# Turning layer 1's attention probabilities with a DMA transpose, under newly ordered plans

## What is computed

```python
x = x + attn(_ln(x) * (scale1 + 1.0) + shift1) * gamma1
h = _gelu_tanh((_ln(x) * (scale2 + 1.0) + shift2) @ Wfc1.T + bfc1)
x = x + (h @ Wfc2.T + bfc2) * gamma2
# attn: 16 heads of 32 features
qn = q / norm(q) * sm; kn = k / norm(k)
p = softmax(einsum('bhqd,bhkd->bhqk', qn, kn) + attn_bias)
o = einsum('bhqk,bhkd->bhqd', p, v) @ Wproj.T + bproj
```

## Time and profile before

| | us |
|---|---|
| median of 3 runs | 2487.38 (2487.06 to 2489.5) |
| the profiled execution | 2486.12 |
| its span, first to last instruction | 2484.3 |
| mean granted TensorE clock | 0.992 of full speed |

### The profile page before, as it was taken

One profiled execution on the slowest core, in us unless ns is written; L12 is line 12 of the kernel. 1 busy time (PEld: TensorE's weight loads), 2 busy tenths in 40 slices (PEclk: granted clock), 3 DMA queues, 4 the chain that ended last, 5 costly groups with the idle time before them and its releaser, 6 DMA issues.

```text
span 2484.3 us, 46028 instructions
## 1 busy us (share of the span) xinstructions
PE 2427.0 (98%) x17878; PEld 1163.2 (47%) x17878; DVE 1345.1 (54%) x2062; ACT 912.9 (37%) x1496; POOL 999.6 (40%) x943
## 2 busy tenths in 40 slices
PE   7699999999999999999999999999999999999999
PEld 4244444444444444444444444454545444454544
DVE  7474251533415234152575585867757586766752
ACT  3343231322313223132343462625445262644542
POOL 2242231332323223132344354645546464555632
PEclk8899999999999999999999999999999999999999
DMA  8762423314132131333443635334252524425230
GB/s 217 208 146 62 97 48 81 67 39 102 41 89 58 42 99 41 90 65 92 133 103 111 151 84 140 70 101 96 72 140 48 156 54 111 102 73 127 60 83 30
DMA packets 311485, 231.50 MB, mean 93 GB/s; under 512 B 227718, under 2 KB 238342, under 8 KB 311308
## 3 DMA queue, kind: packets, MB, share of 16 engines
q1 hardware_dynamic: 311308, 228.89, 37.1%
HBM read 124.08 MB, written 18.75 MB: 57 GB/s over the span
## 4 chain that ended last, share of the span: by engine, by line
PE 81%; DVE 6%; issue 4%; DMA 3%; POOL 3%; ACT 2%; SPq 1%; POOLq 0%; DVEq 0%; ACTq 0%
PE ps_m L1882 46%; PE ps_abef L1882 17%; PE ps_c L1882 5%; PE ps_d L1882 3%; PE ps_abef L2075 2%; PE ps_abef L2071 2%; PE ps_abef L2069 2%; POOL scratch L1278 1%; PE ps_abef L2105 1%; POOL scratch L1274 1%; PE ps_abef L2113 1%; DVE weights L1571 1%; DMA scratch<-mod 1%; PE ps_abef L2094 1%; PE ps_d L1965 1%
## 5 line engine op out<-in xcount | busy, mean ns | idle before, releaser
L1882 PE MATMUL ps_m<-h_mlp,weights 128*128 128x512 f16 x3168 | 723.1, 380 | 8.0 <-DVE scratch L1709 3.6
L1882 PE MATMUL ps_m<-weights,inner 128*128 128x512 f16 x3072 | 681.4, 379 | 0.3 <-POOL inner L1248 0.3
L1248 POOL TENSOR_TENSOR inner<-scratch,inner 128x512 f16<-128x512 f32 x256 | 303.5, 1191 | 466.7 <-ACT inner L1421 466.2
L1882 PEld LDWEIGHTS ps_m<-h_mlp,weights 128*128 128x128 f16 x3168 | 304.1, 98 | 367.5 <-issue 9.2
L1882 PEld LDWEIGHTS ps_m<-weights,inner 128*128 128x128 f16 x3072 | 297.7, 98 | 352.2 <-POOL inner L1248 0.6
L1882 PE MATMUL ps_abef<-h_mlp,weights 128*128 128x512 f16 x1440 | 330.1, 379 | 0.0
L1222 POOL TENSOR_TENSOR scratch<-scratch 128x512 f16<-128x512 f32 x120 | 141.6, 1180 | 410.9 <-ACT scratch L1374 410.1
L1882 PEld LDWEIGHTS ps_abef<-h_mlp,weights 128*128 128x128 f16 x1440 | 137.4, 98 | 164.8 <-issue 4.2
L1421 ACT CAST inner<-scratch 128x512 f16<-128x512 f32 x256 | 156.8, 613 | 106.9 <-DVE scratch L1716 69.0
L1374 ACT CAST scratch<-scratch 128x512 f16<-128x512 f32 x120 | 74.0, 616 | 313.7 <-DMA h_mlp<-scratch 157.7
L1845 DVE SCALAR_TENSOR_TENSOR scratch<-scratch 128x512 f32<-128x512 f32 x128 | 102.1, 799 | 57.0 <-ACT scratch L1510 56.9
(11 more groups left out here) (172 smaller groups left out, 3041.2 us busy)
## 6 DMA issues: line engine op xcount, KB each, us to landing
scratch<-mod SPq DMA_DIRECT2D x128, 256.0 KB, 4.0
x_mlp<-x_attn SPq DMA_DIRECT2D x64, 256.0 KB, 2.4
weights<-gamma SPq DMA_DIRECT2D x128, 128.0 KB, 3.0
scratch<-scratch SPq DMA_DIRECT2D x128, 128.0 KB, 2.7
scratch<-gain SPq DMA_DIRECT2D x112, 128.0 KB, 2.9
x_attn<-x SPq DMA_DIRECT2D x32, 256.0 KB, 2.9
x_mid<-x_mlp SPq DMA_DIRECT2D x32, 256.0 KB, 2.1
x_attn<-x_mid SPq DMA_DIRECT2D x32, 256.0 KB, 3.1
```

The lines of the kernel that those rows point to most:

```text
L1248: nc.gpsimd.tensor_tensor(inner[:, 1, j, :], src, inner[:, 0, j, :], ALU.subtract).then_inc(L.m_lo, 1)
L1882: ins = nc.tensor.matmul(o, left(a, k), right(b, k), start=(first and n == 0), stop=(last and n == len(order) - 1), skip_group_check=True)
```

## The change

Layer 1's turn_p becomes one DMA transpose on SP, as in layer 0, of 16 blocks of 128x128 from `p1` to `pt1`. The PE transposes and the key_major copies are removed; mix, p_hi, turn and the later `up` steps wait for the DMA's semaphore, or no longer for the copies. All eight order tables, and the lists that place set-up steps, have new numbers.

```diff
+                if stage == "turn_p":
+
+                    cut_done, mixed = counts(tile(it, t) + 1, tile(it, t))
+                    sp.wait_ge(s_cond, 1)
+                    sp.wait_ge(L1.p_lo, cut_done)
+                    sp.wait_ge(L1.mixed, mixed)
+                    sp.dma_start(pt1, p1.rearrange("p g h t -> p (g h t)"), transpose=True).then_inc(L1.pt, 16)
...
-                    act.wait_ge(L1.p_turned, n)
+                    act.wait_ge(L1.pt, 16 * n)
                     nc.scalar.copy(p1[:, :, 0, :], e1).then_inc(L1.p_hi, 1)
-                if stage == "key_major":
-                    act.wait_ge(L1.p_turned, n + 1)
-                    act.wait_ge(L1.mixed, n)
-                    nc.scalar.copy(pt1[:, 0:HALF, :], as16(ps_m[2], HALF)).then_inc(L1.pt, 1)
...
-                if stage == "key_major":
-                    dve.wait_ge(L1.p_turned, n + 1)
-                    dve.wait_ge(L1.mixed, n)
-                    nc.vector.tensor_copy(pt1[:, HALF:, :], as16(ps_m[3], HALF)).then_inc(L1.pt2, 1)
...
                     pe.wait_ge(L1.normed, 2 * n + 2)
-                    pe.wait_ge(L1.pt, n)
-                    pe.wait_ge(L1.pt2, n)
+                    pe.wait_ge(L1.masked, n)
...
-                if stage == "turn_p":
-
-                    pe.wait_ge(L1.p_lo, n + 1)
-                    for g in range(HEADS1):
-                        ins = nc.tensor.transpose(as16(ps_m[2 + g // HALF], HALF)[:, g % HALF, :],
-                                                  p1[:, g].rearrange("p h t -> p (h t)"), ident16[:])
-                    ins.then_inc(L1.p_turned, 1)
                 if stage == "mix":
-                    pe.wait_ge(L1.pt, n + 1)
-                    pe.wait_ge(L1.pt2, n + 1)
+                    pe.wait_ge(L1.pt, 16 * (n + 1))
```

A line of a table, before and after, here the place of `mix` in layer 1's steady plan (one number per tile):

```diff
-    "mix": tiles([46.07, 77.91, 116.14, 175.46]),
+    "mix": tiles([52.35, 94.62, 156.69, 264.35]),
```

More of the change, by code:

```diff
@@ new lines @@
+    "p_lo": tiles([50.24, 98.95, 151.71, 237.61]),
+    "scores": tiles([55.71, 92.42, 146.92, 165.18]),
+    "exp": tiles([65.39, 122.48, 149.43, 177.74]),
+    "shift": tiles([69.22, 96.01, 144.90, 168.13]),
+    "turn_p": tiles([70.02, 102.84, 147.08, 168.14]),
+    "p_hi": tiles([72.34, 131.61, 152.35, 188.90]),
+    "mix": tiles([74.10, 116.87, 164.84, 241.80]),
+    "soft": tiles([74.15, 104.92, 145.84, 177.79]),
+    "out": tiles([83.94, 135.98, 201.19, 297.09]),
+    "c_lo": tiles([84.28, 134.13, 164.78, 257.06]),
@@ new lines @@
+    "flip1": tiles([4.21, 40.42, 47.55, 287.22], 1),
+    "shift": tiles([5.20, 56.42, 89.05, 129.62]),
+    "hi1": tiles([8.06, 40.85, 52.36, 409.32], 1),
+    "p_lo": tiles([17.34, 54.45, 90.81, 147.66]),
+    "soft": tiles([21.77, 57.08, 89.25, 142.84]),
+    "exp": tiles([29.70, 54.78, 89.13, 136.52]),
+    "p_hi": tiles([30.83, 60.21, 94.14, 165.41]),
+    "turn_p": tiles([33.00, 69.24, 132.29, 139.25]),
+    "scores": tiles([34.99, 62.77, 88.92, 139.02]),
+    "c_lo": tiles([43.60, 71.20, 101.37, 170.16]),
@@ L213 @@
[L213 to L216 removed]
+    (-296.14, "ang", 0), (-233.76, "ang", 1), (-187.93, "load", "ada4"), (-167.46, "load", "up0"),
@@ new lines @@
+    "proj": tiles([26.36, 56.64, 81.92, 129.62]),
+    "t_hi": tiles([27.78, 60.41, 92.66, 135.24]),
+    "projv": tiles([37.51, 52.82, 83.88, 134.46]),
+    "spread": tiles([43.53, 81.67, 120.41, 188.18]),
+    "t_lo": tiles([44.63, 61.39, 90.17, 135.33]),
+    "mask": tiles([45.55, 69.84, 101.00, 147.82]),
+    "soft": tiles([47.33, 72.92, 104.82, 180.32]),
+    "turn": tiles([48.11, 76.09, 97.29, 138.86]),
+    "exp": tiles([50.29, 75.28, 104.97, 177.01]),
+    "p_hi": tiles([50.36, 82.02, 122.31, 192.56]),
@@ new lines @@
+    "scores": tiles([52.67, 78.28, 114.41, 143.87]),
+    "p_lo": tiles([53.30, 78.53, 106.98, 173.16]),
+    "c_hi": tiles([57.19, 92.99, 178.86, 300.61]),
+    "c_lo": tiles([58.07, 90.92, 187.27, 238.86]),
+    "add": tiles([69.76, 109.55, 183.78, 303.92]),
+    "weigh": tiles([69.80, 112.27, 206.44, 249.60]),
+    "mix": tiles([71.78, 107.22, 163.81, 313.88]),
+    "turn_p": tiles([71.89, 96.15, 129.02, 182.77]),
+    "stat2": tiles([73.34, 132.88, 215.48, 293.15]),
+    "fetch2": tiles([73.74, 161.82, 196.79, 294.84]),
@@ new lines @@
+    "v_lo": tiles([20.26, 41.40, 72.69, 147.51]),
+    "t_lo": tiles([20.77, 57.07, 108.38, 162.69]),
+    "exp": tiles([22.46, 63.26, 135.82, 188.49]),
+    "mask": tiles([26.05, 62.12, 111.25, 164.71]),
+    "turn": tiles([26.20, 57.63, 105.33, 161.50]),
+    "scores": tiles([29.63, 58.06, 119.66, 183.38]),
+    "soft": tiles([31.41, 65.51, 113.90, 187.10]),
+    "spread": tiles([31.42, 69.24, 137.59, 169.31]),
+    "p_hi": tiles([32.35, 67.29, 153.20, 210.50]),
+    "add": tiles([42.31, 93.88, 162.20, 233.90]),
@@ L463 @@
         "bank d": [("out", "weigh")],
-        "banks e and f": [("turn", "t_lo"), ("scores", "mask"), ("turn_p", "key_major")],
+        "banks e and f": [("turn", "t_lo"), ("scores", "mask")],
         "moments": [("stat1", "scale1"), ("stat2", "scale2")],
```

441 lines of the change are left out of this document (193 added, 248 removed), and 118 rows, old and new, of tables (LAST1_AT, SETUP_START0, SETUP_START1, SETUP_TRANS).

## The result

| | before | after |
|---|---|---|
| median, us | 2487.22 (4 runs, 2486.72 to 2489.50) | 2474.48 (4 runs, 2470.26 to 2479.45) |
| span of the profiled execution | 2484.3 | 2477.7 |
| its granted clock | 0.992 | 0.988 |

The ratio is 0.9948, with a 95% interval of 0.9933 to 0.9963: 12.7 us faster. The forecast was 30.8 us faster, so the sign was right, the size less than half, and the time just inside the upper end of the range (2443 to 2476).

The account below looks back on a forecast made before the run. TensorE was taken to bound the loops: 28.8 us won by the removal, 1 at the start, 2 at the seam, less 1 for late landings, made 2487.4 - 30.8 = 2456.6 us; range 2443 to 2476.

Parts of the forecast that it names:

- What bounds the kernel: In the loops TensorE is the bound, 81% of the chain; work taken off it there is won in full.
- The sum: Removal, start, seam and single late landings: 2486.1 - 28.8 - 1 - 2 + 1 = 2455.3; against the median, 2456.6 us.
- The removal: Layer 1's transposes on TensorE cost 0.90 us a tile; over 32 tiles 28.8 us is won.
- The steady blocks: Layer 1's steady blocks become shorter by 3.6 us each, from 142.9 to 139.3 us.
- The DMA: Layer 1, scores to mix: the 16-block transpose lands in about 4.9 us (4.3 to 6.2); no tile waits.
- (a): Layer 1's transpose lands late, near 6.2 us; waits of 1.5 us a block, 10.5 us: 2467 us; chance 0.17.
- rival (b): Layer 1's transpose lands at 7.8 us; waits eat the gain: 2506 us; chance 0.06, shared with anything else above 2492.
- SyncE's queue: In the steady block, fetch2 3 goes out some 7 us after p_lo, hidden by about 3 us.
- the second of the signs: Sign of being wrong, in SyncE's queue: SP holds a fetch back until scale2 waits for it.
- The block's end: Last out to next block's first up: slack 0.3 us, counted at nothing, at worst 1 us in each of 7 blocks.
- Start and seam: New plans: start -1 us (bounds -6 and +8), 1400 to 1600 us -2 (bounds -6 and +6).
- rival (c): The new start and seam lose their +8 and +6 us instead of winning 3: 2474 us; chance 0.08.

Follow-up runs that it names:

- experiment 6: Also spelled old_no_transpose: order tables of before, layer 1's transposition left out altogether, mix reading untransposed probabilities; 2471.3 us against 2488.9 for the kernel before, 0.9928.
- experiment 8: The changed kernel with 16 idle TensorE transposes per layer 1 tile put back (28.8 us in all): 2495.8 us against 2476.0 for the changed kernel.
- experiment 7: The changed kernel with its DMA transpose left out, mix reading untransposed probabilities: 2474.1 us, the change itself having 2474.5 and 2476.0.
- experiment 4: The changed kernel with mix of tiles 2 and 3 one down step earlier in layer 1's steady plan: 2474.3 us.
- experiment 1: The changed code under the order tables of the kernel before, with only SyncE's order adapted: 2515.3 us, 1.0099 of before.

## Why the prediction was wrong, step by step

**What bounds the kernel.** "So the loops are bound by TensorE: work taken off it there is won in full" was the step that failed, and with it the term of 28.8 us. It was read from idle time: under 1 us in 200. That tells that TensorE is the one that is late now, not how close behind it the next chain is. Under the old tables 2.8 of a steady block's 3.6 us could be taken before VectorE was late, and at the seam nothing. Experiments 6 and 8 price the 28.8 us at 17.6 and 19.8. No rival in the prediction had this.

**The sum.** The forecast had -28.8 for the removal, -3 for start and seam, nothing for the DMA, +1 for single late landings: -30.8. The runs have -17.6 for the removal alone (experiment 6), +2.8 for the new plans (experiment 7 against 6) and +0.4 to +1.9 for the DMA (the change against experiment 7), which is no more than the scatter: -14.4 to -12.9, beside -12.7 measured.

**The removal.** The work was 0.90 us a tile, as read: the distance between block starts, less what the waits add to the usual distance of two matmuls, fell from 142.0 us before to 138.4 in the change and 138.4 in old_no_transpose, 3.6 us for four tiles. But I summed it over all 32 tiles, though 8 of them lie in the seam and the first MLP. The kernel before waits 16.4 us there in all (1195 to 1538 us), and the earlier trace rows had shown 7.8 us of idle time for a part of it. By my own reading ("it stands still mainly at the start and at the seam of the layers") those 7.2 us should not have been counted in full. They gave 1.1 in experiment 6 and 3.4 in the change.

**The steady blocks.** 139.3 us forecast, 140.7 measured. From 142.8 less 3.6 us the missing 1.5 us are, start to start on PE in the change's six blocks: 1.1 for the two outs right behind their mix (seen in the order printed before the prediction, and not priced, though c_hi's copy had to fit between), 0.54 for scores of tiles 1 and 3 (0.32 and 0.22), 0.25 on average at the block's end, less 0.4 by which the waits for tile 0's and tile 1's q and k became smaller. Experiment 4 shows that these are not independent: when the 1.1 went, waits at the block's end, slower matmuls behind them and a new wait of turn took as much on average.

**The DMA.** Landing 4.9 taken, 4.3 measured, at the lower end of 4.3 to 6.2. The rooms were right within 0.5 us. The rivals (a) and (b), late landings, did not occur in the steady blocks, and the one landing of 6.3 us at the seam had twice that room. The Trainium skill (VectorE: DVE Perf Modes, "The three transpose paths") gives 1309 ns for one 128x128 transpose by DMA. As a price for each block of a batch the measurement decides against it: 16 blocks in one DMA landed in 4.3 us, 0.27 a block. Waits for the transpose that eat the gain, which is how rival (b) costs time, came in experiment 1, in the steady blocks for want of room and not by late landings.

**SyncE's queue.** I summed issue times and let the fetch go out 7 us after p_lo, hidden by 3. It went out 8.9 us after, since the store and the hand-over ahead of it wait for others, and the scale stands at the edge: it waits up to 1.3 us in the change and 2.73 in experiment 4. This is the second of the signs that the prediction named for being wrong. **The block's end** was counted at 0 with slack 0.3 and up to 1 us at worst. In the change it cost 0.6 and 0.9 us in two of six blocks, up to 2.4 in experiment 4. Slack of 0.3 beside a gain of 3.6 was the warning that time won ahead of it could be lost there.

**Start and seam.** For the start -1 was taken and +4 came out, half of the +8 that rival (c) had there. The bounds, -6 to +8, held it, but the sign was a guess between two unlike orders, and the rows weighed could not decide it. For the order at the seam and in the first MLP -2 was taken. What it gave stays open: of the 3.4 us won there the removal accounts for 1.1 under the old tables and for 5.7 under the new ones.

**The range.** It held the time by 1.5 us, and that is luck: it reached so far up for rivals (a) and (c), and neither of them is what happened.

## What to carry to other kernels

Before counting work taken off the busiest engine as won, look for the second chain: let the engine's work shrink on paper and see who is then late, stage by stage. Where that engine already waits for another, do not count it in full: here it was worth nothing at the seam under one order and all of it under another. A run that leaves the work out altogether prices the removal, for the order it is run in, before anything is built; here it says 17.6 of 28.8 us. And when a step is moved on one in-order engine, move its followers on the others.
